# The last attention block of a four-layer kernel: who adds up the exponentials, and in which order TensorE, VectorE and ScalarE finish the block

## The chip, the cores and the metric

One Trainium2 chip, one core of it. The metric is the device time of one launch in microseconds (us); lower is better. The engines are TensorE (PE, its weight loads PEld), VectorE (DVE), ScalarE (ACT), GpSimd (POOL) and SyncE (SP, here the issuer of most transfers).

## The reference, cut to what matters

Four layers with residuals run over x of shape (1, 2048, 128), all in float32:

```python
x = x + L0_attn(layernorm(x))   # 8 heads; softmax over 2048 keys; this layer ends where the change is
x = x + L0_ffn(layernorm(x))    # gate from the MEAN over all 2048 rows of the normalised x, top 2 of 8 experts
x = x + L1_attn(layernorm(x))   # anchors: softmax over 64 anchors, 16 heads
x = x + L1_ffn(layernorm(x))    # top 2 of 8 experts per row
```

Of the first layer:

```python
scores = einsum('bhsd,bhtd->bhst', q, k) * scale
attn = softmax(scores, axis=-1)           # exp(score - row max) / sum over the 2048 keys
o = einsum('bhst,bhtd->bhsd', attn, v_c)
return o.reshape(b, s, H * DK) @ W_O + b_O
```

and of the second, `pooled = x.mean(axis=1); gate = softmax(pooled @ gate_w.T); top_k(gate, 2)`. Nothing of the second layer's experts can be chosen before all 2048 rows are normalised.

## The kernel before, in words

Every engine has its own instruction stream, written out by hand, and streams meet only at semaphores. The first layer is cut into 32 blocks (`NBLK = 32`): 8 heads (outer) by 4 groups of 512 query rows (inner). Block n, head n // 4, does the following, in 8 slots of two key tiles each:

- `scores(n, t)`: one TensorE matmul gives the scores of 128 keys (tile t of 16) by 512 queries; `exponential(n, t)` on ScalarE writes `prob[:, tile, :]`, a ring of 16 tiles, so one whole block fits.
- `weighted` / `weigh(n, tiles)`: `val` times `prob`, 32 output columns per matmul, so four tiles are worked by four matmuls side by side, into bank U. When all 16 are in, `sums(n)` on ScalarE copies the bank to `u_sb[n % 4]`, and `output(n)` on TensorE multiplies by the folded projection into a bank.
- The softmax denominators: for blocks up to 30, GpSimd, VectorE and adding DMAs reduce the 16 `prob` tiles to a `part` buffer, and `totals(n)` sums over partitions with matmuls against `ones_v`; `sums_out(n)` copies to `den_sb`, a small DMA turns it to `den`. For the last block (31), `last_totals(g)`, g = 0 to 3, does the whole sum on TensorE: four groups of four 512-wide matmuls directly over `prob`, accumulated in bank 6. `sums_out(31)` copies the bank to `den_sb`, and `last_denominators()` turns it with four matmuls.
- `denominators(n)` and `accumulate(n)` on VectorE: reciprocal, then X = out * rden + X in four instructions.

The ends of blocks 28 to 31 are each the last word on one quarter (batch b = 0 to 3, 512 rows) of X, so the second layer's normalisation `ln0` starts there, batch by batch: `ln0_stats(b)` (VectorE, 8 instructions), `ln0_pool(b)` (GpSimd: variance plus epsilon, power), `ln0_norm(b)` (VectorE, 4 instructions, writes `hn`), `ln0_pe(b)` (TensorE, 4 transposes), `ln0_act(b)` (ScalarE copies to `hT` and accumulates the row sums `hsum[:, b]`). The mean over all rows is the sum of two parts. For batches 0 to 2, VectorE adds the three columns of `hsum`; that instruction waits for `ln0_act(2)` and stands in front of `ln0_norm(3)` on VectorE. For batch 3, TensorE sums `hn` against `ones_v` directly ("the pooled matmuls", line 1816 of the profile), behind a `spin`, that is, a number of matmuls whose result nobody reads. Then VectorE adds the parts, TensorE forms the gate's logits, VectorE takes the top two, and the experts' weights are picked.

TensorE's order in block 31 before the change: scores 12 and 13; `weighted(31, 0)` (tiles 0 to 7); `last_totals(0)`, `last_totals(1)`; scores 14 and 15; `output(30)`; `last_totals(2)`; `ln0_pe(1)`; `weigh` tiles 8 to 11; `last_totals(3)`; `weigh` tiles 12 to 15; `last_denominators`; `output(31)`; small transposes of the anchors, the gate and `up0`; `ln0_pe(2)`; the eight transposes of `w_out` (line 1781); `anchor_weights(0)` and `(1)` (line 1790); `spin(8)`; the pooled matmuls.

Lines of the profile used below: 1540 scores, 658 exponentials, 1584 `weigh`, 1604 `totals`, 1615 `last_totals`, 1624 `last_denominators`, 1568 `output`, 367 `ln0_pe`, 373 `ln0_act`, 361 `ln0_norm`, 328 and 335 `ln0_stats`, 341 and 343 `ln0_pool`, 1127 `late_sums` (the two wide additions of block 30 on VectorE), 1159 `accumulate`, 1249 the addition of `hsum`, 641 `sums_out(31)`, 721 `anchors_hi`, 1474 `spin`. A float32 matmul appears as two records, so four matmuls of a group are eight.

Of the kernel before, what the change touches and what calls it, by code (L numbers as in the profile page):

```python
# [5 lines left out]
ALU = mybir.AluOpType  # L6
# [12 lines left out]
def build_kernel(nc, d, out):  # L19

    S, D = d["L0_attn_h_t"].shape[1:]
    NT = S // P
    NB = S // BLK
    C = d["L0_attn_W_DQ"].shape[1]
# [8 lines left out]
    with ctx:  # L33
# [6 lines left out]
        ps = ctx.enter_context(nc.psum_tensor("ps", [P, 8, BLK], F32))  # L40
# [359 lines left out]
        u_sb = [sums_sb[:, 0], sums_sb[:, 1]] + [w_oT[:, :, :].rearrange("p h d -> p (h d)")[:, x * BLK:(x + 1) * BLK] for x in range(2)]  # L400
        part = [part_sb[:, 0], part_sb[:, 1]] + [t.rearrange("p (x h) d -> p x (h d)", x=NG) for t in (w_v[:, :, :], hn[:, :, :])]
        with nc.sbuf_tensor("pT", [P, HP, S], F32) as pT:
            pass
# [49 lines left out]
        with nc.Block() as block:  # L453
# [105 lines left out]
            def _(act):  # L559
# [125 lines left out]
                for n in range(NBLK):  # L685
                    for t in range(NT):
# [16 lines left out]
                        if n == NBLK - 1 and t == 10:  # L703
                            ln0_act(act, 0, 3)
                ln0_act(act, 1, 4)
                sums_out(NBLK - 1)
                sums(NBLK - 1)

# [7 lines left out]
                act.copy(up_x[:, :, :], ps[:, 7, :].rearrange("p (j n) -> p j n", j=E // 2)).then_inc(s_upx, 1)  # L716
                ln0_act(act, 2, 3)

# [18 lines left out]
                anchors_hi(0)  # L737
                anchors_hi(1)
                act.wait_ge(s_gv, 2)
                act.activation(g8[:, EXPD, :], g8[:, TOP, :], ACT.Exp, bias=g1[:, 0:1], accum_out=g1[:, 1:2]).then_inc(s_ge, 1)  # L740
# [318 lines left out]
            def _(dve):  # L1059
# [59 lines left out]
                def late_sums(n, j):  # L1119
# [7 lines left out]
                    dve.tensor_tensor(part[n % 4], part[n % 4], prob[:, at:at + NG, :], ALU.add).then_inc(s_pair, 1)  # L1127

                def key_biases(m, bank):
                    heads = slice(4 * m, 4 * (m + 1))  # L1130
                    dve.wait_ge(s_kb_ps, m + 1)
                    dve.tensor_scalar(kcol[:, heads], ps[:, bank, KB_AT + 4 * m:KB_AT + 4 * (m + 1)], unit[:, E_SH:E_SH + 1], None,
                                      ALU.add).then_inc(s_kb, 1)
                    dve.wait_ge(s_kb, 2 * m + 1)
                    dve.tensor_scalar(kcol_m[:, heads], kcol[:, heads], unit[:, M_KEY:M_KEY + 1], None, ALU.mult).then_inc(s_kb, 1)
# [66 lines left out]
                for n in range(NBLK):  # L1202
                    for slot in range(CPB):
# [27 lines left out]
                        if n == NBLK - 1:  # L1231
                            if slot == 0:
                                ln0_norm(dve, 0)
                            elif slot == 3:
                                denominators(n - 2)
                                accumulate(n - 2)
                                ln0_stats(dve, 1)
                            elif slot == 5:
                                ln0_norm(dve, 1)
                            elif slot == 7:  # L1240
                                denominators(n - 1)
                                accumulate(n - 1)
                                ln0_stats(dve, 2)
                ln0_norm(dve, 2)
                denominators(NBLK - 1)
                accumulate(NBLK - 1)
                ln0_stats(dve, 3)
                dve.wait_ge(ln0["hT"], NB + 3)
                dve.tensor_reduce(hsum[:, NB:NB + 1], hsum[:, 0:NB - 1], AX.X, ALU.add).then_inc(s_pooled, 1)
# [209 lines left out]
            def _(pe):  # L1459
# [148 lines left out]
                def last_totals(g):  # L1608

                    n = NBLK - 1  # L1610
                    if g == 0:
                        bank_read(("sums", n))
                    pe.wait_ge(s_exp, NT * n + NG * (g + 1))
                    for x in range(NG):
                        last = pe.matmul(ps[C * x:C * (x + 1), BANK["sums", n], :], ones_v[:, :], prob[:, (NT * n + NG * g + x) % RING, :],
                                         start=(g == 0), stop=(g == NG - 1))
                    if g == NG - 1:
                        last.then_inc(s_ones, 1)
# [82 lines left out]
                for n in range(NBLK):  # L1701
                    for slot in range(CPB):
# [34 lines left out]
                        if slot == 6 and n == NBLK - 3:  # L1737
                            totals(n - 2)
                        if slot == 6 and n == NBLK - 1:
                            last_totals(0)  # L1740
                            last_totals(1)
                        if slot == 1 and n >= 1:
# [5 lines left out]
                        if n == NBLK - 1:  # L1748
# [6 lines left out]
                            elif slot == 7:  # L1755
                                output(n - 1)
                                last_totals(2)
                                bank_read(("norm", 1))
                                ln0_pe(pe, 1, 4)
                                weigh(n, range(2 * NG, 3 * NG))  # L1760
                last_totals(3)
                weigh(NBLK - 1, range(3 * NG, NT))


# [9 lines left out]
                last.then_inc(s_up_ps, 1)  # L1774
                pe.wait_ge(ln0["hT"], NB + 1)
                ln0_pe(pe, 2, 3)

# [34 lines left out]
                anchor_weights(1)  # L1812
                spin(8, 6)
                pe.wait_ge(ln0["hn"], 2 * NT)
# [296 lines left out]
```

## Time and profile before

| | |
|---|---|
| device time, median of 3 runs | 721.29 us (720.11 to 721.71) |
| device time of the profiled execution | 719.99 us |
| its span (first to last instruction) | 718.3 us |
| TensorE busy | 698.3 us (97% of the span) |
| VectorE / GpSimd / ScalarE busy | 582.4 / 563.6 / 460.3 us |
| granted TensorE clock, mean | 0.999 |
| block 31, scores 0 to start of the pooled matmuls | 453.00 to 480.52 us of the span |

Times inside the kernel are counted from the start of the span. The chain that ended last is TensorE for 71% of the span, GpSimd for 11%, VectorE for 7%. A start time of one instruction of an in-order engine subtracted from the next one's gives what the first costs the stream; the busy time of a row can be longer, since neighbours overlap.

### The profile page before, as it was taken

The numbers are of one execution on the slowest core, as the hardware profiler recorded it, in microseconds if no ns is written. First come the engines' busy times: TensorE is split into PE (matmuls) and PEld (weight loads), VectorE is DVE, ScalarE is ACT, GpSimd is POOL, SyncE is SP. The second block draws the span as 40 slices with busy tenths as digits, with TensorE's granted clock in tenths as the row PEclk, the third lists the DMA queues.
The fourth block names the chain that finished last, engine by engine and source line by source line (L and its number), as shares of the span: only waits on it lengthen the run. The fifth ranks groups of instructions, "written<-read, shape, count | busy, mean of one in ns | idle before, by whom it ended". The sixth has DMA issues, their size and how long they took to land.

```text
span 718.3 us, 12481 instructions
## 1 busy us (share of the span) xinstructions
PE 698.3 (97%) x4280; PEld 470.6 (66%) x4280; DVE 582.4 (81%) x1213; ACT 460.3 (64%) x1069; POOL 563.6 (78%) x466
## 2 busy tenths in 40 slices
PE   8999999999999999999999999999899999999997
PEld 7665556566566566566666656476566599778885
DVE  8878888988988898898889888756978536878885
ACT  4357776776776777767767766655677822465553
POOL 6468999999999999999999997415688761446674
PEclk9999999999999999999999999999999999999999
DMA  6313768778678688687687683040000000032431
GB/s 152 93 38 67 146 126 155 132 137 151 124 148 150 116 154 153 113 156 146 121 153 139 133 155 67 1 121 2 1 2 0 2 1 1 1 89 81 141 104 30
DMA packets 42595, 68.34 MB, mean 95 GB/s; under 512 B 14872, under 2 KB 24105, under 8 KB 38692
## 3 DMA queue, kind: packets, MB, share of 16 engines
q0 software_dynamic: 15680, 52.96, 38.8%
q1 hardware_dynamic: 25572, 14.47, 7.6%
q8 instruction: 34, 0.56, 0.3%
q10 hardware_dynamic: 1280, 0.12, 0.1%
q14 instruction: 29, 0.24, 0.1%
HBM read 13.35 MB, written 1.10 MB: 20 GB/s over the span
## 4 chain that ended last, share of the span: by engine, by line
PE 71%; POOL 11%; issue 7%; DVE 7%; DMA 3%; ACT 2%; POOLq 0%; ACTq 0%; DVEq 0%
PE ps L1540 16%; PE ps L1584 15%; PE ps L1526 15%; POOL hid_lo L1055 5%; PE ps L1953 4%; PE ps L1568 4%; POOL nrm L1035 2%; DVE mx L1109 2%; PE ps L1993 2%; PE ps L1995 2%; PE ps L1994 2%; POOL hid L1035 1%; DMA w_v<-prob 1%; PE ps L1604 1%; PE ps L1513 1%
## 5 line engine op out<-in xcount | busy, mean ns | idle before, releaser
L1109 DVE TENSOR_REDUCE mx<-ps 128x1 f32<-128x512 f32 x492 | 303.1, 682 | 47.9 <-PE ps L1526 47.8
L658 ACT ACTIVATE prob<-ps 128x512 f32<-128x512 f32 x512 | 261.8, 627 | 21.3 <-PE ps L1540 16.2
L1540 PE MATMUL ps<-q_cols,key 128*128 128x512 f32 x512 | 210.3, 414 | 2.3 <-ACT prob L658 1.7
L1526 PE MATMUL ps<-key,q_rows 128*128 128x512 f32 x512 | 202.8, 400 | 0.8 <-DVE key L1095 0.4
L1540 PEld LDWEIGHTS ps<-q_cols,key 128*128 128x128 f32 x512 | 95.4, 187 | 73.9 <-issue 34.1
L1584 PE MATMUL ps<-prob,val 128*32 128x512 f32 x1024 | 123.3, 598 | 0.0
L1526 PEld LDWEIGHTS ps<-key,q_rows 128*128 128x128 f32 x512 | 95.7, 188 | 18.8 <-DVE mx L1103 1.4
L960 POOL TENSOR_TENSOR pair<-prob 128x512 f32<-128x512 f32 x60 | 104.8, 1770 | 4.0 <-ACT prob L658 4.0
L946 POOL TENSOR_TENSOR part<-prob 128x512 f32<-128x512 f32 x64 | 96.5, 1820 | 5.7 <-ACT prob L658 5.6
L1055 POOL TENSOR_TENSOR hid_lo<-hid,hid_hi 128x512 fp32r<-128x512 f32 x44 | 61.6, 1409 | 38.6 <-ACT hid_hi L826 38.6
L1584 PEld LDWEIGHTS ps<-prob,val 128*32 128x32 f32 x1024 | 26.7, 109 | 51.1 <-issue 47.4
L946 POOL TENSOR_TENSOR w_v<-prob 128x512 f32<-128x512 f32 x32 | 48.1, 1808 | 4.4 <-ACT prob L658 4.4
L810 ACT ACTIVATE act_g<-ps 128x512 f32<-128x512 f32 x44 | 26.4, 599 | 32.9 <-PE ps L1995 32.6
L946 POOL TENSOR_TENSOR hn<-prob 128x512 f32<-128x512 f32 x28 | 43.5, 1975 | 2.0 <-ACT prob L658 2.0
L1159 DVE SCALAR_TENSOR_TENSOR X<-ps,rden,X 128x128 f32<-128x128 f32 x128 | 36.0, 344 | 7.4 <-PE ps L1568 4.2
L778 ACT ACTIVATE pT<-ps 128x128 f32<-128x128 f32 x128 | 33.7, 278 | 10.6 <-PE ps L1930 10.6
L967 POOL TENSOR_TENSOR part<-part,pair 128x1024 f32<-128x1024 f32 x16 | 39.1, 2445 | 0.0
L1425 DVE TENSOR_TENSOR prod<-ps,act_g 128x512 f32<-128x512 f32 x44 | 30.1, 685 | 10.8 <-PE ps L1995 8.5
L341 POOL TENSOR_SCALAR vare<-mv 128x4 f32<-128x4 f32 x12 | 4.7, 392 | 41.5 <-DVE mv L335 41.2
L639 ACT COPY den_sb<-ps 128x128 f32<-128x128 f32 x31 | 8.3, 266 | 43.4 <-PE ps L1604 42.6
L1993 PE MATMUL ps<-hT_hi,w_hi 128*128 128x512 f32 x88 | 35.5, 403 | 0.0
L1435 DVE TENSOR_TENSOR hid<-g_all,prod 128x512 f32<-128x512 f32 x26 | 30.6, 1177 | 5.0 <-POOL hid_lo L1055 4.2
(301 smaller groups left out, 1319.4 us busy)
## 6 DMA issues: line engine op xcount, KB each, us to landing
part<-prob POOLq DMA_DIRECT2D x16, 1024.0 KB, 7.1
part<-part POOLq DMA_DIRECT2D x14, 512.0 KB, 8.1
w_v<-prob POOLq DMA_DIRECT2D x7, 1024.0 KB, 7.1
hn<-prob POOLq DMA_DIRECT2D x7, 1024.0 KB, 7.0
part<-part POOLq DMA_DIRECT2D x14, 256.0 KB, 7.4
w_v<-w_v POOLq DMA_DIRECT2D x7, 512.0 KB, 8.0
hn<-hn POOLq DMA_DIRECT2D x7, 512.0 KB, 8.0
g_all<-g_rows SPq DMA_DIRECT2D x9, 256.0 KB, 3.2
```

What stands on the lines that cost most here:

```text
L658: act.activation(prob[:, g % RING, :], ps[:, g % 3, :], ACT.Exp, scale=SCALE).then_inc(s_exp, 1)
L778: act.activation(pT[:, 4 * m + q, u * P:(u + 1) * P], ps[:, 6 + m, q * P:(q + 1) * P], ACT.Copy, accum_out=apart[:, 4 * m + q, u:u + 1]).t ...
L946: pool.tensor_tensor(part[n % 4][:, g, :], tiles(n, 2 * g, 1)[:, 0, :], tiles(n, 2 * g + 1, 1)[:, 0, :], ALU.add).then_inc(s_sum, 1)
L960: pool.tensor_tensor(pair[:, j, :], tiles(n, t, 1)[:, 0, :], tiles(n, t + 1, 1)[:, 0, :], ALU.add).then_inc(s_pair, 1)
L967: pool.tensor_tensor(p, p, pair[:, :, :], ALU.add).then_inc(s_sum, 1)
L1055: pool.tensor_tensor(hid_lo[:, n % 4, :], hid[:, n % 2, :], hid_hi[:, n % 4, :].bitcast(F32), ALU.subtract).then_inc(s_hlo, 1)
L1109: dve.tensor_reduce(mx[:, n % 2, c % TPB, at:at + 1], ps[:, BANK["rows", 2 * lin + j], :], AX.X, ALU.max).then_inc(s_mrd, 1)
L1159: last = dve.scalar_tensor_tensor(out=xt, in0=ps[:, BANK["out", n], i * P:(i + 1) * P], scalar=rden[:, n % 2, i:i + 1], in1=xt, op0=ALU.mu ...
L1526: pe.matmul(ps[:, BANK["rows", 2 * lin + j], :], q_rows[:, k, i * P:(i + 1) * P], key[:, h % KBUF, c0:c0 + BLK], start=True, stop=True).th ...
L1540: pe.matmul(ps[:, g % 3, :], key[:, n // NB % KBUF, t * P:(t + 1) * P], q_cols[:, n % NB, :], start=True, stop=True).then_inc(s_sc, 1)
L1584: last = pe.matmul(ps[C * x:C * (x + 1), U, :], val[:, t, :], prob[:, (NT * n + t) % RING, :], start=(t < NG), stop=(t >= NT - NG))
L1993: pe.matmul(out_ps, w[0], x_hi, start=start, stop=False)
```

## The change

- VectorE adds tiles 0 to 3 and 4 to 7 of block 31 (`last_sums(0)`, behind `ln0_norm(1)`), then tiles 8 to 11 (`last_sums(1)`), into `last_part`, which is `part_sb[:, 1]`. Each is one addition of 128 x 2048.
- TensorE's `last_totals` has two groups instead of four: tiles 12 to 15 from `prob`, then `last_part`. Both stand behind all `weigh` calls of the block.
- `output(30)` moves from in front of the last `ln0_pe(1)` and `weigh` calls to behind them.
- ScalarE copies `sums(31)` before `sums_out(31)`.
- `ln0_norm(2)` on VectorE goes from before `denominators(31)` to behind `ln0_stats(3)`; `ln0_pe(2)` on TensorE and `ln0_act(2)` on ScalarE go behind the anchor weights.
- The spin in front of the pooled matmuls is `spin(4)` instead of `spin(8)`.

```diff
--- before.py
+++ after.py
@@ -399,6 +399,7 @@
 
         u_sb = [sums_sb[:, 0], sums_sb[:, 1]] + [w_oT[:, :, :].rearrange("p h d -> p (h d)")[:, x * BLK:(x + 1) * BLK] for x in range(2)]
         part = [part_sb[:, 0], part_sb[:, 1]] + [t.rearrange("p (x h) d -> p x (h d)", x=NG) for t in (w_v[:, :, :], hn[:, :, :])]
+        last_part = part[(NBLK - 1) % 4 - 2]
         with nc.sbuf_tensor("pT", [P, HP, S], F32) as pT:
             pass
         act_g = sb("act_g", [P, 2, BLK])
@@ -703,8 +704,8 @@
                         if n == NBLK - 1 and t == 10:
                             ln0_act(act, 0, 3)
                 ln0_act(act, 1, 4)
+                sums(NBLK - 1)
                 sums_out(NBLK - 1)
-                sums(NBLK - 1)
 
 
                 act.wait_ge(s_an_ps, 1)
@@ -714,7 +715,6 @@
                 act.activation(gate0T[:, :], ps[:, 0, AT_GATE:AT_GATE + E], ACT.Copy, scale=1.0 / S).then_inc(s_an, 1)
                 act.wait_ge(s_up_ps, 1)
                 act.copy(up_x[:, :, :], ps[:, 7, :].rearrange("p (j n) -> p j n", j=E // 2)).then_inc(s_upx, 1)
-                ln0_act(act, 2, 3)
 
                 def anchors_hi(m):
                     act.wait_ge(s_wa_ps, m + 1)
@@ -736,6 +736,7 @@
                     act.copy(w_oT[:, 4 * m:4 * (m + 1), :], ps[:, 1 + m, :].rearrange("p (h n) -> p h n", h=4)).then_inc(s_wo, 1)
                 anchors_hi(0)
                 anchors_hi(1)
+                ln0_act(act, 2, 3)
                 act.wait_ge(s_gv, 2)
                 act.activation(g8[:, EXPD, :], g8[:, TOP, :], ACT.Exp, bias=g1[:, 0:1], accum_out=g1[:, 1:2]).then_inc(s_ge, 1)
                 act.activation(warm[:, :], ones_row[:, 0:1], ACT.Gelu)
@@ -1125,6 +1126,18 @@
                         dve.wait_ge(s_pair, 2 * n + j)
                     dve.wait_ge(s_exp, NT * n + NG * (3 + j))
                     dve.tensor_tensor(part[n % 4], part[n % 4], prob[:, at:at + NG, :], ALU.add).then_inc(s_pair, 1)
+
+                def last_sums(j):
+
+                    n = NBLK - 1
+                    at = [(NT * n + NG * x) % RING for x in range(3)]
+                    if j == 0:
+                        first = prob[:, at[0]:at[0] + NG, :]
+                    else:
+                        first = last_part
+                        dve.wait_ge(s_pair, 2 * n + 1)
+                    dve.wait_ge(s_exp, NT * n + NG * (2 + j))
+                    dve.tensor_tensor(last_part, first, prob[:, at[j + 1]:at[j + 1] + NG, :], ALU.add).then_inc(s_pair, 1)
 
                 def key_biases(m, bank):
                     heads = slice(4 * m, 4 * (m + 1))
@@ -1237,14 +1250,16 @@
                                 ln0_stats(dve, 1)
                             elif slot == 5:
                                 ln0_norm(dve, 1)
+                                last_sums(0)
                             elif slot == 7:
+                                last_sums(1)
                                 denominators(n - 1)
                                 accumulate(n - 1)
                                 ln0_stats(dve, 2)
-                ln0_norm(dve, 2)
                 denominators(NBLK - 1)
                 accumulate(NBLK - 1)
                 ln0_stats(dve, 3)
+                ln0_norm(dve, 2)
                 dve.wait_ge(ln0["hT"], NB + 3)
                 dve.tensor_reduce(hsum[:, NB:NB + 1], hsum[:, 0:NB - 1], AX.X, ALU.add).then_inc(s_pooled, 1)
                 ln0_norm(dve, 3)
@@ -1610,11 +1625,15 @@
                     n = NBLK - 1
                     if g == 0:
                         bank_read(("sums", n))
-                    pe.wait_ge(s_exp, NT * n + NG * (g + 1))
+                        at = (NT * n + 3 * NG) % RING
+                        tiles = prob[:, at:at + NG, :]
+                    else:
+                        pe.wait_ge(s_pair, 2 * n + 2)
+                        tiles = last_part
                     for x in range(NG):
-                        last = pe.matmul(ps[C * x:C * (x + 1), BANK["sums", n], :], ones_v[:, :], prob[:, (NT * n + NG * g + x) % RING, :],
-                                         start=(g == 0), stop=(g == NG - 1))
-                    if g == NG - 1:
+                        last = pe.matmul(ps[C * x:C * (x + 1), BANK["sums", n], :], ones_v[:, :], tiles[:, x, :],
+                                         start=(g == 0), stop=(g == 1))
+                    if g == 1:
                         last.then_inc(s_ones, 1)
 
                 def last_denominators():
@@ -1736,9 +1755,6 @@
                             totals(n - 3)
                         if slot == 6 and n == NBLK - 3:
                             totals(n - 2)
-                        if slot == 6 and n == NBLK - 1:
-                            last_totals(0)
-                            last_totals(1)
                         if slot == 1 and n >= 1:
                             weighted(n - 1, 1)
                         if slot == 1 and n == NBLK - 3:
@@ -1753,13 +1769,13 @@
                                 bank_read(("norm", 0))
                                 ln0_pe(pe, 0, 3)
                             elif slot == 7:
-                                output(n - 1)
-                                last_totals(2)
+                                weigh(n, range(2 * NG, 3 * NG))
                                 bank_read(("norm", 1))
                                 ln0_pe(pe, 1, 4)
-                                weigh(n, range(2 * NG, 3 * NG))
-                last_totals(3)
                 weigh(NBLK - 1, range(3 * NG, NT))
+                output(NBLK - 2)
+                last_totals(0)
+                last_totals(1)
 
 
                 pe.wait_ge(s_exp, NT * NBLK)
@@ -1772,8 +1788,6 @@
                 for j in range(E // 2):
                     last = pe.transpose(ps[:, 7, j * P:(j + 1) * P], up0[:, 2 * j:2 * (j + 1), :].rearrange("p e c -> p (e c)"), ident[:, :])
                 last.then_inc(s_up_ps, 1)
-                pe.wait_ge(ln0["hT"], NB + 1)
-                ln0_pe(pe, 2, 3)
 
                 for m in range(2):
                     for q in range(4):
@@ -1810,7 +1824,9 @@
                 pe.wait_ge(s_an, 3)
                 anchor_weights(0)
                 anchor_weights(1)
-                spin(8, 6)
+                pe.wait_ge(ln0["hT"], NB + 1)
+                ln0_pe(pe, 2, 3)
+                spin(4, 6)
                 pe.wait_ge(ln0["hn"], 2 * NT)
                 for t in range(NT - TPB, NT):
                     last = pe.matmul(ps[:, 0, AT_POOL:AT_POOL + C], hn[:, t, :], ones_v[:, :], start=(t == NT - TPB), stop=(t == NT - 1))
```

## Rows read from the trace of the kernel before

**Rows 1.** The page: the span.

```profile
span 718.3 us, 12481 instructions
```

**Rows 2.** Chain that ended last, in order of time: start, us, what.

```profile
497.56 0.14 issue
```

**Rows 3.** Timeline, TensorE, 463 to 481: start, us, instructions merged.

```profile
463.42 1.92 PE L1584 MATMUL ps<-prob,val 128*32 128x512 f32 x16
465.16 1.90 PE L1615 MATMUL ps<-prob,ones_v 128*32 128x512 f32 x16
466.99 0.73 PE L1540 MATMUL ps<-q_cols,key 128*128 128x512 f32 x2
467.56 1.05 PE L1568 MATMUL ps<-proj,w_oT 128*128 128x128 f32 x8
468.54 1.06 PE L1615 MATMUL ps<-prob,ones_v 128*32 128x512 f32 x8
469.54 0.65 PE L367 MATMUL ps<-ident,hn 128*128 128x128 f32 x4
470.12 1.06 PE L1584 MATMUL ps<-prob,val 128*32 128x512 f32 x8
471.01 1.04 PE L1615 MATMUL ps<-prob,ones_v 128*32 128x512 f32 x8
471.86 1.04 PE L1584 MATMUL ps<-prob,val 128*32 128x512 f32 x8
472.84 1.04 PE L1624 MATMUL ps<-mean_v,den_sb 128*128 128x1 f32 x8
473.75 1.14 PE L1568 MATMUL ps<-proj,w_oT 128*128 128x128 f32 x8
...
475.64 0.60 PE L367 MATMUL ps<-ident,hn 128*128 128x128 f32 x4
476.08 1.04 PE L1781 MATMUL ps<-ident,w_out 128*128 128x128 f32 x8
476.95 1.95 PE L1790 MATMUL ps<-anchors,emb 128*128 128x128 f32 x16
478.74 1.95 PE L1474 MATMUL ps<-ident 128*128 128x128 f32 x16
480.52 0.98 PE L1816 MATMUL ps<-ones_v,hn 128*128 128x32 f32 x8
```

**Rows 4.** Timeline, VectorE; in brackets idle time before and its releaser.

```profile
453.44 4.58 DVE L1127 TENSOR_TENSOR w_v<-w_v,prob 128x2048 f32<-128x2048 f32 x2
...
464.06 1.12 DVE L361 TENSOR_SCALAR hn<-X,mv,rstd 128x128 f32<-128x128 f32 x4 [1.48 <-POOL rstd L343]
...
474.93 1.13 DVE L1159 SCALAR_TENSOR_TENSOR X<-ps,rden,X 128x128 f32<-128x128 f32 x4 [0.82 <-PE ps L1568]
...
477.16 0.12 DVE L1249 TENSOR_REDUCE hsum<-hsum 128x1 f32<-128x3 f32 x1
...
478.72 1.12 DVE L361 TENSOR_SCALAR hn<-X,mv,rstd 128x128 f32<-128x128 f32 x4 [1.44 <-POOL rstd L343]
```

**Rows 5.** Timeline, ScalarE.

```profile
470.72 0.19 ACT L373 ACTIVATION_READ_ACCUMULATOR hT<-ps 128x1 f32 x1
...
472.11 0.59 ACT L641 COPY den_sb<-ps 128x512 f32<-128x512 f32 x1 [1.20 <-PE ps L1615]
...
478.94 0.59 ACT L721 CAST w_a_hi<-ps 128x512 fp32r<-128x512 f32 x1 [0.31 <-PE ps L1790]
```

**Rows 6.** Instructions of line 341, 445 to 485: ns shortest/median/longest, first and last start.

```profile
L341 POOL TENSOR_SCALAR vare<-mv x4: 229/230/2177, 453.6 to 477.3; 128x4 f32<-128x4 f32 x4
```

**Rows 7.** Timeline, TensorE: the first spin, and a gap at 515.7.

```profile
1.59 6.08 PE L1474 MATMUL ps<-ident 128*128 128x128 f32 x28 [1.59 <-POOL ident L872]
...
517.65 0.66 PE L1930 MATMUL ps<-ident,hid 128*128 128x128 f32 x4 [1.94 <-POOL hid L1035]
```

**Rows 8.** Windows: stretch, then PE, PEld, DVE, ACT, POOL busy, granted clock, DMA.

```profile
515.00:518.00 3.00, 1.06 (x7) 0.59 (x6) 2.93 (x5) 2.49 (x13) 2.93 (x3) 1.00 0.00 0
```

## The prediction

> **What bounds the kernel now.** I read the page first: the span is 718.3 us [rows 1] and TensorE is busy for nearly all of it, so only what TensorE does, or waits for, can count. I then followed the chain that ended last through the stretch of the change. From 453 to 480.5 us it is TensorE with hardly a break; its one crossing to another engine in the part I use is the step from VectorE's `hn` to TensorE's transposes, 0.14 us [rows 2]. The timeline of TensorE gives the cost of each step of block 31 as differences of starts [rows 3]. VectorE's and ScalarE's timelines [rows 4, 5] say what else must be ready. Two things are to be seen. First, `output(31)` starts at 473.75 right behind `last_denominators` at 472.84. Secondly, the pooled matmuls start at 480.52, when `spin(8)` is through, but the last `hn` tile was ready at 478.72 + 1.12 = 479.84 [rows 3, 4]: TensorE's queue, not VectorE, sets that start, with 0.68 to spare on VectorE's side. Everything behind 480.52 keeps its instructions and their order, and everything up to 463.42 does too. So the whole forecast is one question: when do the pooled matmuls start after the change?
>
> **Part 1, TensorE up to output(31).** Start at 463.42. I add the steps in the new order, with durations from [rows 3]. A group of four `weigh` or four `ones` matmuls (8 records) costs 0.87 (1.74 for 16 records, 463.42 to 465.16). If a plain matmul follows, it costs 0.09 to 0.13 more (465.16 to 466.99 is 1.83 for 16; 468.54 to 469.54 is 1.00; 471.86 to 472.84 is 0.98).
>
> - `weigh` tiles 0 to 7: 1.83. Two scores: 0.57 (466.99 to 467.56). `weigh` 8 to 11: 1.00. `ln0_pe(1)`: 0.58. `weigh` 12 to 15: 0.98. `output(30)`: 0.98. First group of totals: 0.87. Second group, to its end: 1.04. Sum 7.85, end at 471.27.
> - Now TensorE must wait for ScalarE, which it did not before. ScalarE started its copy 0.06 behind the end of the last group (471.01 + 1.04 = 472.05, copy at 472.11) and took 0.59 [rows 3, 5]. Then 0.14 back to TensorE. `last_denominators` starts at 471.27 + 0.06 + 0.59 + 0.14 = 472.06, against 472.84.
>
> The two groups taken from TensorE are worth 1.74, but 0.79 of wait on the copy takes the place of work that used to hide it, and one more switch to plain matmuls takes the rest. Net gain 0.78: `output(31)` starts at 472.97. The order of ScalarE's two copies costs nothing: `u_sb` is copied while TensorE does `output(30)` and the totals, and it would delay TensorE only if it ended after 472.8; `weigh` 12 to 15 starts at 467.40 by this count and ends at 468.44, and the copy behind it takes 0.6.
>
> **Part 2, the wide additions.** The same operation stands in block 30: two additions of 128 x 2048 in 4.58 us [rows 4]. They ran beside exponentials and `weigh` as they will here. `ln0_norm(1)` ends at 464.06 + 1.12 = 465.18, so the second addition ends at 469.76. TensorE wants it at 470.23; with 0.14 for the crossing, 0.33 is left. `accumulate(30)` comes behind the additions, at about 470, and needs `output(30)`, which now ends at about 469.4. It and `ln0_stats(2)` take 2.23, as the same pair at 474.93 to 477.16 [rows 4], so VectorE is free at 472.2, before it is wanted for `denominators(31)` at about 473.1. GpSimd's pass over batch 2 then ends before 474. These additions are hidden; without the slack each us of delay would be a us of TensorE.
>
> **Part 3, the third normalisation.** `accumulate(31)` starts 0.78 earlier, at 474.15, `ln0_stats(3)` is issued out by 474.15 + 2.23 = 476.38 [rows 4]. Before, `ln0_norm(3)` then waited only for GpSimd. Now comes a chain:
>
> - `ln0_norm(2)`, 1.12: ends 477.50.
> - TensorE: crossing 0.14 gives 477.64. Is TensorE free? From `output(31)` to the transposes of `w_out` are the 1.89 us of 473.75 to 475.64 (`ln0_pe(2)`'s 0.44 is gone from here), so 474.86; these take 0.87 (476.08 to 476.95), so 475.73; the first anchor weights wait for the copy of `up0` on ScalarE, by my count until 475.79; 1.79 for all anchor weights (476.95 to 478.74) gives 477.58 [rows 3]. Both arrive together. Transposes 477.64 to 478.29.
> - ScalarE: the second `anchors_hi` started 1.99 behind the anchor weights' start (478.94 against 476.95) and took 0.59 [rows 3, 5], so it ends at 475.79 + 1.99 + 0.59 = 478.37. `ln0_act` took 0.72 from the end of the transposes to the end of the accumulator read (469.54 + 0.65 = 470.19 to 470.91) [rows 3, 5]; with the short wait behind `anchors_hi` it ends at 479.05.
> - VectorE: the crossing from ScalarE's accumulator read is in no row by itself. Its bounds are nothing and the 0.14 of [rows 2]; I take 0.04, near the 0.04 to 0.06 of the other crossings into ScalarE here. `hsum`'s addition 0.12, then `ln0_norm(3)` 1.12: ends at 480.33. Crossing 0.14: the pooled matmuls can start at 480.47.
> - TensorE itself: transposes 0.44, then `spin(4)`, half of the 1.78 of `spin(8)` (478.74 to 480.52): free at 477.64 + 0.44 + 0.89 = 478.97. It waits 1.5 us.
>
> So the pooled matmuls start at 480.47 instead of 480.52. **The sum is -0.05 us.** The 0.78 gained at `output(31)`, the 0.44 taken out of TensorE's queue and the 0.89 of shorter spin all lie in front of a chain that starts with `ln0_norm(2)` and is as long as all of them together. `ln0_norm(3)` would be free of it were `hsum`'s addition not in front of it.
>
> The other moves are free: the loads of the last layer's weights, behind the same semaphore as `ln0_stats(3)`, start 0.78 earlier, and the next user is far behind them. Of unknown costs, two more switches of TensorE between kinds of matmul may cost 0 to 0.2 together; the four crossings of part 3 might be 0.1 off each, and the accumulator read may or may not be what `hsum` waits for (0.1 less). The likeliest case's own range is -0.3 to +0.5.
>
> Profiled, the kernel took 719.99 for a span of 718.3; the span becomes 718.25 and that execution 719.94. The median of 3 runs is 1.30 above the profiled execution, and I carry that over: 721.29 - 0.05 = 721.2.
>
> **The clock.** The gap of about 1.5 us in front of the pooled matmuls is new. In the gap of 1.94 us in front of 517.65 [rows 7] the granted clock stayed 1.00 [rows 8], the upper level (2.4 GHz), and the transposes behind it took 0.66, as the 0.65 of 469.54 [rows 3]. The Trainium skill, "TensorE: Matmul & The Clock Gate", section "Why this matters for your kernels", warns that a long idle gap between bursts of matmuls sends the array back to half rate, which speaks against a halved spin; by it TensorE behind 480.5 would start at 1.2 GHz, which is the rival priced below. The rows show a longer gap without it.
>
> **Rivals.**
>
> *Part of the gain arrives (faster).* If `hsum`'s wait does not bind, `ln0_norm(3)` waits for GpSimd only: 478.72 - 0.78 = 477.94, ends 479.06, pooled matmuls at 479.20, -1.32 us: 719.97. The code puts the wait there, so the full amount cannot come; a fraction can, if the crossings are shorter. For: TensorE's own queue is 1.5 us ahead. Cases from -0.3 to -1.3, about 720.7.
>
> *The chain through hT is longer than counted (slower).* TensorE and ScalarE both arrive at `ln0_pe(2)` and `ln0_act(2)` within 0.1 us of being free. If the anchor weights or the copies in front of them slip by 0.3 and each crossing costs 0.14, the pooled matmuls start 0.4 to 1.0 late: about 722.0.
>
> *The additions are late (slower, on the other side).* It decides from 0.33 us on. GpSimd's variance step took 2.18 us beside block 30's additions, against 0.23 otherwise [rows 6]: on a shared path one side can be held for 1.95. If each of the new additions were held so, `last_sums(1)` ends 3.9 late, less 0.33: +3.6, 724.9. Against: GpSimd has nothing to do between 464.0 and 471, and block 30's additions, beside that very step, took their 4.58.
>
> *The clock drops.* The first spin of the program took 6.08/28 = 0.217 us per record, against 1.78/16 = 0.111 in the spin at 478.74 [rows 3, 7]. If the 4 us behind 480.5 ran at that pace: +3.9, 725.2.
>
> **How the numbers follow.** Dead heat (-0.3 to +0.5): 0.60. Part of the gain: 0.20. Longer chain: 0.14. Late additions: 0.03. Clock: 0.02. Something else: 0.01. What a measurement of this kernel can tell from no change is about 0.2%, 1.44 us. Even the full gain of 1.32 stays inside it, and so does the longer chain; but medians of 3 runs scatter (720.11 to 721.71 before), and a real -0.8 can be read as -1.5. From the part-gain case, plus scatter, faster 0.11; from the late additions, the clock, and scatter on the longer chain, slower 0.09; same 0.80. The range of 8 in 10 takes the cases from -1.3 to +1.0 with a little scatter: 719.9 to 722.4.
>
> **What the changed profile would show.** `output(31)` at about 473.0, with TensorE idle 0.8 in front of `last_denominators` waiting for `den_sb`; second addition over by 469.8 and no TensorE wait on it; `ln0_pe(2)` at 477.6 released by VectorE or just behind the anchor weights; `hsum`'s addition at 479.1 released by ScalarE, where before it waited for nothing; the pooled matmuls at 480.4 to 480.6, now released by VectorE's `hn` after an idle gap of TensorE instead of by the spin. The prediction is wrong if the pooled matmuls start before 480.1 or after 481.0, or if the stretch behind them changes its length.

## The result: slower, with the pooled matmuls where they were

| | before | after |
|---|---|---|
| median, 18 runs each | 720.95 us | 726.53 us |
| lowest, highest | 719.39, 722.4 | 721.37, 731.43 |
| ratio | | 1.0068, 95% interval 1.005 to 1.0085 |
| profiled execution: span, mean granted clock | 718.3 us, 0.999 | 724.5 us, 0.988 |

(The ratio on record lies at that of the means, 1.0068; that of the medians is 1.0077.) An execution more than 1.5% above the fastest of its kernel is left out of a ratio as disturbed, which happened once, to the 732.52 us of `g_spin7` below. The change makes the kernel slower by 0.7%. The time is outside the stated range, 719.9 to 722.4. Of the 18 executions of the changed kernel, 4 took 721.4 to 721.9 us at a mean clock of 0.997, one 723.3 at 0.995, and the other 13 took 726.0 to 731.4 at 0.982 to 0.988.

The page of the changed kernel, its first lines and the row of the granted clock by slice (tenths of full speed, 9 for 90% or more, 40 slices):

```profile
span 724.5 us, 12435 instructions
...
PEclk9999999999999999999999999988999999999999
```

TensorE's timeline of the changed kernel, from the first `weigh` of block 31 to the picks, which answers to [rows 3] (1599 is `weigh`, 1555 scores, 1634 `last_totals`, 1643 `last_denominators`, 1583 `output`, 1804 the anchor weights, 1489 `spin`, 1832 the pooled matmuls, 1810 the first values of the third layer):

```profile
463.33 1.92 PE L1599 MATMUL ps<-prob,val 128*32 128x512 f32 x16
465.19 0.73 PE L1555 MATMUL ps<-q_cols,key 128*128 128x512 f32 x2
...
468.43 1.16 PE L1583 MATMUL ps<-proj,w_oT 128*128 128x128 f32 x8
469.52 1.07 PE L1634 MATMUL ps<-prob,ones_v 128*32 128x512 f32 x8
470.40 1.04 PE L1634 MATMUL ps<-part,ones_v 128*32 128x512 f32 x8
472.24 1.02 PE L1643 MATMUL ps<-mean_v,den_sb 128*128 128x1 f32 x8 [0.80 <-ACT den_sb L642]
473.12 1.14 PE L1583 MATMUL ps<-proj,w_oT 128*128 128x128 f32 x8
...
477.81 0.60 PE L367 MATMUL ps<-ident,hn 128*128 128x128 f32 x4
478.24 1.06 PE L1489 MATMUL ps<-ident 128*128 128x128 f32 x8
480.45 1.08 PE L1832 MATMUL ps<-ones_v,hn 128*128 128x32 f32 x8 [1.15 <-DVE hn L361]
...
482.49 1.22 PE L1810 MATMUL ps<-w_oT,emb 64*128 64x128 f32 x4
```

The reader is to see two new idle gaps, 0.80 us in front of `last_denominators` and 1.15 in front of the pooled matmuls, the pooled matmuls at 480.45 against 480.52, and in the last row four records that take 1.22 us. In the kernel before the same four, same shapes, read:

```profile
482.47 0.71 PE L1796 MATMUL ps<-w_oT,emb 64*128 64x128 f32 x4
```

VectorE of the changed kernel, against [rows 4]:

```profile
465.01 2.29 DVE L1140 TENSOR_TENSOR part<-prob 128x2048 f32<-128x2048 f32 x1
467.33 2.29 DVE L1140 TENSOR_TENSOR part<-part,prob 128x2048 f32<-128x2048 f32 x1
...
476.53 1.08 DVE L361 TENSOR_SCALAR hn<-X,mv,rstd 128x128 f32<-128x128 f32 x4
479.21 0.16 DVE L1264 TENSOR_REDUCE hsum<-hsum 128x1 f32<-128x3 f32 x1 [1.60 <-ACT hT L373]
479.29 1.11 DVE L361 TENSOR_SCALAR hn<-X,mv,rstd 128x128 f32<-128x128 f32 x4
```

Now the time, cut into three stretches: from the first `weigh` of block 31, from the pooled matmuls to the first up projection (490.32 before, 496.61 after), and the rest. Windows of the kernel before, then of the changed one (columns: stretch, its length, busy us of PE, PEld, DVE, ACT, POOL with instructions, granted clock, DMA share, GB/s):

```profile
463.40:480.50 17.10, 17.10 (x145) 11.00 (x145) 8.21 (x39) 8.37 (x21) 3.53 (x7) 1.00 0.20 57
480.50:490.30 9.80, 9.55 (x68) 7.00 (x66) 4.11 (x18) 4.40 (x11) 0.00 (x0) 1.00 0.46 125
490.30:718.30 228.00, 216.15 (x1167) 168.87 (x1166) 167.20 (x350) 128.62 (x409) 142.88 (x109) 1.00 0.12 36
```

```profile
463.30:480.50 17.20, 15.25 (x122) 9.47 (x121) 12.61 (x41) 8.40 (x21) 3.53 (x7) 1.00 0.23 70
480.50:496.60 16.10, 15.85 (x66) 11.29 (x66) 4.11 (x18) 4.40 (x11) 0.00 (x0) 0.58 0.24 62
496.60:724.50 227.90, 216.15 (x1167) 168.88 (x1166) 167.23 (x350) 128.44 (x409) 142.79 (x109) 0.99 0.12 36
```

All of the loss is in the middle stretch: the same work, 66 weight loads in both, takes 16.10 us instead of 9.80, at a granted clock of 0.58 on average. The same view cut finer shows the edges:

```profile
482.00:482.50 0.50, 0.50 (x5) 0.33 (x5) 0.42 (x4) 0.12 (x1) 0.00 (x0) 0.97 1.20 291
482.50:483.00 0.50, 0.50 (x3) 0.50 (x3) 0.43 (x3) 0.48 (x3) 0.00 (x0) 0.50 1.20 291
...
495.00:496.00 1.00, 1.00 (x2) 0.00 (x0) 0.10 (x1) 0.00 (x0) 0.00 (x0) 0.50 0.00 0
496.00:497.00 1.00, 1.00 (x6) 0.69 (x6) 0.00 (x0) 0.29 (x2) 0.00 (x0) 0.94 0.00 0
```

From 482.5 to about 496.1 TensorE ran at the lower level (0.50, 1.2 GHz), though it was busy throughout; the fall came 2 us after the gap had ended. Just before it, TensorE had idled for 1.15 us and then, after the pooled matmuls, for 0.25 us in front of the gate's logits, which it did in the kernel before too.

### The profile page after: what moved, and what is told of

Read it like the earlier page. It is cut to its first block, busy times and chain, and to the rows that moved or that the text cites. A ratio compares the mean times of both kernels' runs of the same rounds, so it can differ in the third digit from the quotient of the medians.

```text
span 724.5 us, 12435 instructions
## 1 busy us (share of the span) xinstructions
PE 701.7 (97%) x4256; PEld 471.7 (65%) x4256; DVE 586.9 (81%) x1215; ACT 460.1 (63%) x1069; POOL 563.3 (78%) x466
## 4 chain that ended last, share of the span: by engine, by line
PE 72%; POOL 10%; issue 7%; DVE 5%; DMA 3%; ACT 2%; POOLq 0%; ACTq 0%; DVEq 0%
PE ps L1555 17%; PE ps L1599 15%; PE ps L1541 15%; POOL hid_lo L1056 5%; PE ps L1969 4%; PE ps L1583 4%; POOL nrm L1036 2%; PE ps L2009 2%; PE ps L2011 2%; PE ps L2010 2%; DVE mx L1110 1%; POOL hid L1036 1%; DMA w_v<-prob 1%; PE ps L1619 1%; PE ps L1528 1%
```

## The experiments

Theory 1: the new idle gaps of TensorE lower the clock, the one in front of the pooled matmuls above all. Rivals: the new order of the totals, with its wait for `den_sb`, lowers it whatever stands in front of the pooled matmuls; or the gap alone, in the old order, does nothing. Each kernel was timed beside the kernel before on the same chip. "From weigh" is the time from the first `weigh` of block 31 to the pooled matmuls in the profiled execution: it shows what the schedule alone does. "Fall" is the time that the clock stayed at 0.50 behind the pooled matmuls in the profiled execution, worked out from windows of it.

The last two columns count executions by their mean granted clock. The 13 profiles say what that mean stands for: the four with a mean of 0.998 or more show no fall up to 714 us, close to the end of the span, and the nine with 0.997 or less each show one (3.4 us of it: 0.996 or 0.997; 6.8 us: 0.995; 10 us at the start of the program: 0.992; 13.6 us: 0.988; 20.5 us: 0.984). So "high", 0.998 or more, stands for no fall, and "low", 0.989 or less, for a long one or several. Of the 104 executions of the kernel before that ran beside these kernels, 64 were high and none was low; their lowest was 0.991.

| kernel | gaps, us | from weigh, us | fall, us | ratio, 95% interval | high | low |
|---|---|---|---|---|---|---|
| before | none | 17.10 | none | 1 | 64 of 104 | 0 of 104 |
| the change | 0.80 + 1.15 | 17.12 | 13.6 | 1.0068 (1.005 to 1.0085) | 0 of 18 | 13 of 18 |
| a_spin10 | 0.80 | 17.14 | none | 1.0006 (0.9991 to 1.0022) | 5 of 12 | 0 of 12 |
| g_spin7 | 0.80 + 0.48 | 17.12 | 3.4 | 1.0022 (1.000 to 1.0044) | 3 of 12 | 1 of 12 |
| h_spin0 | 0.80 + 2.04 | 17.12 | 20.5 | 1.0081 (1.0051 to 1.0112) | 0 of 6 | 4 of 6 |
| b_spin0 | 0.98 | 16.47 | 3.4 | 1.0036 (1.0016 to 1.0055) | 0 of 12 | 3 of 12 |
| c_sums_only | 0.80 | 16.56 | none | 1.0012 (0.999 to 1.0034) | 5 of 12 | 0 of 12 |
| d_norm_only | 1.15 | 17.67 | 6.8 | 1.0058 (1.0036 to 1.0079) | 0 of 12 | 4 of 12 |
| k_den_spin | 1.15 | 17.05 | none | 1.0042 (1.0023 to 1.0061) | 1 of 12 | 1 of 12 |
| e_hsum_last | 0.80 | 15.93 | none | 0.999 (0.9971 to 1.0009) | 6 of 12 | 0 of 12 |
| f_hsum_spin6 | 0.80 | 16.26 | none | 0.9998 (0.9974 to 1.0022) | 3 of 12 | 0 of 12 |
| i_fill | 0.17 | 16.17 | none | 0.9983 (0.997 to 0.9997) | 9 of 12 | 0 of 12 |
| i_fill_again | 0.17 | 16.16 | none | 0.9985 (0.9968 to 1.0001) | 6 of 12 | 0 of 12 |

**The size of the gap, with the changed order kept.** Three kernels differ from the change in one number (g_spin7 has `spin(7, 6)`, h_spin0 no spin):

```diff
-                spin(4, 6)
+                spin(10, 6)
```

> The changed kernel with ten spin matmuls in place of four in front of the pooled matmuls, nothing else. Theory 1 (the idle gap of 1.15 us that TensorE has there, after the 0.80 us wait for den_sb, makes the clock fall to half about 2 us later): the gap closes, the pooled matmuls start at 480.4 to 480.5 as before, the granted clock stays 1.00 from 482 to 496 and the mean is 0.999; time 720.9, that is 0.2 us around the kernel before. Rival (the clock falls because of the thinner TensorE work of the new order, the 0.80 us wait for den_sb above all, not because of the gap ahead of the pooled matmuls): the clock still falls, time 724 to 727.

> The changed kernel with a spin of seven instead of four: the gap ahead of the pooled matmuls is 0.5 us instead of 1.15, the pooled matmuls start at 480.45 as before. If the share of executions with a fallen clock grows with the gap: between the ten-matmul version (ratio 1.0006) and the change (1.0068), about 1.002 to 1.004. If there is an edge, one of the two.

> The changed kernel without any spin: the gap ahead of the pooled matmuls is 2.0 us, the pooled matmuls start at 480.45. Theory 1: the clock falls at least as often and as early as in the change, ratio 1.007 to 1.010, no execution with a mean clock of 0.999 or more. Rival (the gap is not the cause, what the four spin matmuls do is nothing): as the change, 1.0068.

The pooled matmuls start equally late in all four, 17.12 to 17.14 us after the first `weigh`. Only the gap differs, and the ratio follows it: 1.0006, 1.0022, 1.0068, 1.0081 for no gap there, 0.48, 1.15 and 2.04. The two smallest overlap in their intervals and so do the two largest; the jump between 0.48 and 1.15 us is clear. Theory 1 holds, and the rival falls: a_spin10 has the totals and the wait for `den_sb` exactly as the change, and no low execution. g_spin7 has one low execution, but its profiled one, with a mean of 0.997, shows that the small gap does something too:

```profile
481.41 1.08 PE L1832 MATMUL ps<-ones_v,hn 128*128 128x32 f32 x8 [0.48 <-DVE hn L361]
```

```profile
484.00:486.00 2.00, 2.00 (x13) 1.67 (x12) 1.42 (x6) 1.80 (x4) 0.00 (x0) 0.61 0.34 82
```

h_spin0 is not clearly worse than the change by ratio, but all six of its executions had a mean clock of 0.992 or less (of the change 13 of 18), and in its profile the fall came earlier:

```profile
480.00:482.00 2.00, 1.35 (x8) 1.27 (x8) 0.59 (x3) 0.00 (x0) 0.00 (x0) 0.81 1.14 349
482.00:484.00 2.00, 1.75 (x9) 1.32 (x9) 1.01 (x7) 1.07 (x3) 0.00 (x0) 0.50 1.08 261
```

The profiled execution of a_spin10 happened to be its slowest (725.77 us). Windows of it show where, in the first 20 us of the program, and not in this stretch:

```profile
8.00:20.00 12.00, 11.13 (x42) 7.23 (x43) 7.49 (x32) 5.49 (x13) 5.11 (x16) 0.57 0.54 132
...
482.00:500.00 18.00, 17.11 (x125) 13.66 (x124) 8.58 (x42) 8.25 (x20) 4.22 (x7) 1.00 0.43 122
```

So there is a second place at which the clock can fall, at the start, where all these kernels have the same instructions. It may also explain part of the scatter of the kernel before (up to 726 us, mean clock down to 0.991), though no profile of the kernel before shows it. A third place comes with `i_fill` below.

**The gap alone, in the old order.**

```diff
                 anchor_weights(1)
-                spin(8, 6)
```

> The kernel before without its spin of eight matmuls, nothing else. The pooled matmuls are then released by VectorE's hn at 479.84 and start at 479.98, 0.54 us earlier, behind an idle gap of TensorE of about 1.1 us. Theory 1 (a gap of about 1 us here is enough): the granted clock falls to 0.50 for 10 to 13 us in most executions, time 724 to 727. Rival (the gap alone is not enough, the rest of the new order is needed too): clock stays 0.999, time 720.4.

The schedule gained 0.63 us (16.47 against 17.10), and the time got 0.36% worse. Its profiled execution is one of the mild ones (mean clock 0.997) and shows a short fall:

```profile
479.38 1.08 PE L1815 MATMUL ps<-ones_v,hn 128*128 128x32 f32 x8 [0.98 <-DVE hn L361]
```

```profile
482.00:484.00 2.00, 2.00 (x13) 1.69 (x12) 1.42 (x6) 1.78 (x4) 0.00 (x0) 0.62 1.05 254
484.00:486.00 2.00, 2.00 (x13) 2.00 (x11) 0.15 (x1) 0.00 (x0) 0.00 (x0) 0.53 0.00 0
486.00:488.00 2.00, 2.00 (x13) 1.12 (x12) 0.76 (x2) 0.75 (x2) 0.00 (x0) 1.00 0.04 8
```

So a gap of 1 us in front of the pooled matmuls is enough by itself. My expectation of a fall of 10 to 13 us in most executions was too much: 3 of 12 were low. But all 12 had a mean clock of 0.997 or less, where 64 of 104 of the kernel before had more, so a shorter fall, as in this profile (3.4 us), is likely in most.

**The change in halves.** c_sums_only keeps the additions, the totals and the order of TensorE and takes back the moves of batch 2 and the spin:

```diff
 # VectorE, from the change
+                ln0_norm(dve, 2)
                 denominators(NBLK - 1)
                 accumulate(NBLK - 1)
                 ln0_stats(dve, 3)
-                ln0_norm(dve, 2)
 # TensorE
                 last.then_inc(s_up_ps, 1)
+                pe.wait_ge(ln0["hT"], NB + 1)
+                ln0_pe(pe, 2, 3)
...
                 anchor_weights(1)
-                pe.wait_ge(ln0["hT"], NB + 1)
-                ln0_pe(pe, 2, 3)
-                spin(4, 6)
+                spin(8, 6)
```

(`ln0_act(2)` goes back likewise.) d_norm_only is the other half, the same lines in the other direction, made in the kernel before.

> The changed kernel with the moves of the third normalisation and the shorter spin undone: the wide additions, the two groups of totals, output(30) behind the last weights and the order of the two copies stay; norm, transposes and copy of batch 2 stand where they stood, and the spin has eight matmuls. The wait for den_sb of 0.80 us stays, the gap ahead of the pooled matmuls is gone. Norm of batch 2 on VectorE now waits for GpSimd until about 473.6 and holds accumulate(31) to about 474.8, so little is gained: the pooled matmuls start at about 480.0. Theory 1: granted clock 0.999, time 720.2 to 720.9. Rival (the new order of totals and its wait on den_sb lower the clock): clock falls to 0.50 behind 482, time 724 to 727.

> The kernel before with only the moves of the third normalisation and the spin of four: norm of batch 2 behind the last statistics, its transposes and its copy behind the anchor weights. The chain through hsum then starts 0.78 us later than in the changed kernel: hsum's addition at about 480.0, pooled matmuls at about 481.2, 0.7 us later than before, behind a gap of about 1.2 us. Theory 1: the clock falls as in the changed kernel, time 725 to 728. Rival (the totals and the den_sb wait are needed): clock 0.999, time 721.6.

The first half gains 0.54 us of schedule, as expected, and has no low execution. Its median, 721.37, is no better than that of the kernel before, 721.15: a gain of 0.54 us is below what 12 executions can tell, and it is above the 720.2 to 720.9 that I had expected. The second half costs 0.57 us of schedule by itself (0.7 expected) and brings the gap of 1.15; 4 of 12 executions were low and none was high. The slowdown belongs to the second half.

**Does the wait for den_sb count too?** k_den_spin puts three spin matmuls into it and leaves the later gap:

```diff
+                spin(3, 1)
                 last_denominators()
```

> The changed kernel with three spin matmuls in the 0.80 us wait for den_sb ahead of last_denominators; the gap of 1.15 us ahead of the pooled matmuls stays. If only the later gap counts: ratio as in the change, 1.006 to 1.008. If the two gaps add up: about that of the kernel before without its spin (one gap of 1 us), 1.0036.

1.0042, with 1 low execution of 12 against 13 of 18, and the schedule as before. That points to the two gaps adding up, as does d_norm_only (1.15 alone, 4 of 12); the intervals of the ratios overlap, so it is likely, not shown. With 1 high execution of 12 the clock fell somewhere in nearly every one; what seems rarer with the earlier gap filled is a long fall. Its profiled execution has the gap of 1.15 us and no fall behind it (its 0.996 comes from a later place, see `i_fill`):

```profile
481.11 1.08 PE L1833 MATMUL ps<-ones_v,hn 128*128 128x32 f32 x8 [1.15 <-DVE hn L361]
```

```profile
484.00:486.00 2.00, 2.00 (x20) 1.88 (x17) 1.58 (x7) 1.50 (x4) 0.00 (x0) 1.00 0.19 45
486.00:490.00 4.00, 4.00 (x28) 2.71 (x27) 1.08 (x4) 1.72 (x5) 0.00 (x0) 1.00 0.03 6
```

So a gap of 1.15 us does not lower the clock in every execution.

**Taking hsum out of the chain.** The prediction had named `hsum`'s addition, in front of `ln0_norm(3)`, as what eats the gain. e_hsum_last swaps the two:

```diff
                 ln0_norm(dve, 2)
+                ln0_norm(dve, 3)
                 dve.wait_ge(ln0["hT"], NB + 3)
                 dve.tensor_reduce(hsum[:, NB:NB + 1], hsum[:, 0:NB - 1], AX.X, ALU.add).then_inc(s_pooled, 1)
-                ln0_norm(dve, 3)
```

> The changed kernel with the addition of hsum behind ln0_norm(3) on VectorE instead of in front of it; spin of four. ln0_norm(3) then waits only for GpSimd (478.05) and ends at 479.2, the pooled matmuls start at 479.3 to 479.4, 1.1 us earlier than in the kernel before, and TensorE's gap ahead of them is 0.2 us instead of 1.15. Theory 1 (the gap lowers the clock): clock as in the kernel before, time about 719.9 where no clock falls, ratio 0.997 to 0.999. Rival (four spin matmuls and the new order are too thin whatever the gap): clock still falls, 724 or more.

f_hsum_spin6 is the same with `spin(6, 6)`:

> As e_hsum_last with a spin of six: TensorE is busy until 479.57, so no gap ahead of the pooled matmuls, which start at 479.6, 0.9 us earlier than in the kernel before. Theory 1: clock as in the kernel before, ratio 0.998 to 0.999. Rival (thin order): clock falls.

The schedule is 1.17 and 0.84 us shorter than before, as expected, with no gap in front of the pooled matmuls in either and no low execution. e_hsum_last keeps the four spin matmuls of the change, so it was the gap that lowered the clock and not the small number of them. The ratios, 0.999 and 0.9998, cannot be told from 1.

**Both gaps filled.** i_fill has the swap of e_hsum_last and real work in the wait for `den_sb`:

```diff
+                pe.wait_ge(s_usb, NBLK)
+                pe.transpose(ps[0:A, 0, 0:A], anchor[:, :], ident[0:A, 0:A])
+                pe.transpose(ps[:, 0, AT_GATE:AT_GATE + E], gate0[:, :], ident[0:E, 0:E]).then_inc(s_an_ps, 1)
+                for j in range(E // 2):
+                    last = pe.transpose(ps[:, 7, j * P:(j + 1) * P], up0[:, 2 * j:2 * (j + 1), :].rearrange("p e c -> p (e c)"), ident[:, :])
+                last.then_inc(s_up_ps, 1)
                 last_denominators()
                 output(NBLK - 1)
-                pe.transpose(ps[0:A, 0, 0:A], anchor[:, :], ident[0:A, 0:A])
...
                 anchor_weights(1)
+                spin(3, 6)
                 pe.wait_ge(ln0["hT"], NB + 1)
                 ln0_pe(pe, 2, 3)
-                spin(4, 6)
+                spin(6, 6)
```

> hsum's addition last as in e_hsum_last, and both gaps of TensorE filled: the transposes of the anchors, the gate and up0 go in front of last_denominators, into the 0.80 us wait for den_sb (behind a wait for u_sb), three spin matmuls stand in front of ln0_pe(2), six behind it. TensorE is then busy without a gap from 463 to the pooled matmuls at 479.5, 0.9 to 1.0 us earlier than in the kernel before. Theory 1: clock as in the kernel before, ratio 0.998 to 0.999, and not better than e_hsum_last if a gap of 0.8 and one of 0.2 do nothing; better by up to 0.001 if they matter.

> A repeat of i_fill, whose interval (0.997 to 0.9997) came close to 1. If the gain is real: ratio 0.9975 to 0.9995 again, from 0.9 us less up to the pooled matmuls and fewer executions with a lowered clock. If it was chance: about 1.000.

TensorE's timeline of i_fill, where the 0.80 us wait is gone and one gap of 0.17 is left:

```profile
471.00 1.04 PE L1634 MATMUL ps<-part,ones_v 128*32 128x512 f32 x8
471.98 0.24 PE L1785 MATMUL ps<-ident,anchor 64*64 64x64 f32 x1
...
472.80 1.01 PE L1643 MATMUL ps<-mean_v,den_sb 128*128 128x1 f32 x8
...
478.30 0.63 PE L367 MATMUL ps<-ident,hn 128*128 128x128 f32 x4 [0.17 <-DVE hn L361]
478.77 1.50 PE L1489 MATMUL ps<-ident 128*128 128x128 f32 x12
480.11 0.98 PE L1834 MATMUL ps<-ones_v,hn 128*128 128x32 f32 x8
```

0.9983 and, repeated, 0.9985: medians 719.70 and 720.01 against 720.74 and 720.56. The first interval excludes 1 and the second just reaches it. This version is 0.15% faster than the kernel before and 0.8% faster than the change; the first is within the 0.2% that I had called no change, and is as large as the 0.93 us of its schedule (16.17 against 17.10).

The repeat shows one thing more. The prediction had taken the gap of 1.94 us in front of 517.65 as proof that such a gap is harmless. The two runs are the same program, and their profiled executions differ right there. TensorE's rows and a window, first of i_fill, then of i_fill_again:

```profile
517.22 0.66 PE L1948 MATMUL ps<-ident,hid 128*128 128x128 f32 x4 [1.94 <-POOL hid L1036]
521.26 0.60 PE L1948 MATMUL ps<-ident,nrm 128*128 128x128 f32 x4
518.00:521.00 3.00, 3.00 (x13) 1.90 (x12) 2.10 (x4) 2.84 (x17) 2.37 (x2) 1.00 0.00 0
```

```profile
516.63 0.66 PE L1948 MATMUL ps<-ident,hid 128*128 128x128 f32 x4 [1.94 <-POOL hid L1036]
522.33 0.60 PE L1948 MATMUL ps<-ident,nrm 128*128 128x128 f32 x4
518.00:521.00 3.00, 3.00 (x9) 1.86 (x8) 1.54 (x3) 2.40 (x13) 1.78 (x1) 0.50 0.00 0
```

In the second the clock fell for 3.4 us, and the way to the next transposes took 5.70 us instead of 4.04: a short fall costs 1.7 us. The same gap is followed by the same fall in the profiles of f_hsum_spin6 and k_den_spin (1.95 us, 5.71 and 5.69), three of 13 in all.

## Why the prediction was wrong

Its own question, when the pooled matmuls start, was answered rightly, step by step; times below in us, predicted and measured, the measured ones being 0.09 earlier from the start (463.33 against 463.42).

| step | predicted | measured |
|---|---|---|
| second addition ends | 469.76 | 467.33 + 2.29 = 469.62 |
| wait for `den_sb` in front of `last_denominators` | 0.79 | 0.80 |
| `output(31)` starts | 472.97 | 473.12 |
| `ln0_norm(2)` ends | 477.50 | 476.53 + 1.08 = 477.61 |
| `ln0_pe(2)` starts | 477.64 | 477.81 |
| `hsum`'s addition starts | 479.09 | 479.21 |
| `ln0_norm(3)` ends | 480.33 | 480.40 |
| pooled matmuls start | 480.47 | 480.45 |
| TensorE idle in front of them | 1.5 | 1.15 |

- **Part 1.** The gain at `output(31)` was 0.78 predicted; from the first `weigh` it is 10.33 before (473.75 - 463.42) and 9.79 after, 0.54. `output(30)` behind the last weights took 1.09 instead of 0.98, and the two scores 0.66 (465.19 to 465.85) instead of 0.57; the wait for `den_sb` was right. The size is a bit off, the mechanism right.
- **Part 2.** Right. The additions took 2.29 each, and TensorE did not wait for them. The rival of late additions did not occur.
- **Part 3.** Right. The chain through `hsum` gave back what had been gained, and e_hsum_last showed the other side of it: with the swap the pooled matmuls come 1.17 us earlier, as the rival "part of the gain arrives" had worked out in full (1.32).
- **"Everything behind 480.52 keeps its instructions and their order."** True, but I took from it that the stretch keeps its length. It took 6.30 us more.
- **"The clock."** This is the step that failed. I had seen the new gap and taken one gap of 1.94 us at 517.65, with no fall behind it [rows 7, 8], for proof that 1.5 us is harmless, and gave the rival a chance of 0.02. That one execution proves nothing even for its own place: behind the same gap the clock fell in 3 of the 13 profiles, and in one of two executions of the same program (i_fill and i_fill_again). In place of "harmless" the runs showed: with a gap of about 1 us the clock falls in most executions (59 of 60 with a gap of 0.98 us or more had a mean clock of 0.997 or less, against 40 of 104 of the kernel before), and it stays down for 3.4 to 13.6 us, 20.5 behind the gap of 2.04. Why it is short in one execution and long in another stays open.
- **The price of that rival** was +3.9 us, on a guess that the low clock lasts for 4 us. It lasted 13.6 us (482.5 to 496.1), and work that took 9.80 us took 16.10: +6.3 in the profiled execution, +5.6 in the median. The rival's 725.2 is near the measured 726.53, but with a length that was a guess.
- **"spin(4), half of spin(8)".** I booked the eight spin matmuls of before as a wait in TensorE's queue, 0.68 us too long. They also kept TensorE busy up to the release of the pooled matmuls. Taking out four (0.89), with all that stands in front of them 0.54 earlier and the release where it was, is what opened the gap. (It is 1.15 and not the predicted 1.5 because `ln0_pe(2)` started 0.17 late and the last spin matmul ends 0.17 behind the half of `spin(8)` that I had counted.)

The Trainium skill, "TensorE: Matmul & The Clock Gate", section "Why this matters for your kernels", warns of idle gaps between bursts of matmuls; the prediction cited it and set it aside. The gaps that it warns of are longer than any here, so by its words the 1.15 us gap was no danger either; the measurement decides. The runs agree with its direction: the clock went to the lower of its two levels (1.2 GHz) after gaps of 0.48 to 2.04 us, and in the profile of a_spin10, with the gap closed, it stayed at 1.00.

## What to carry to other kernels

Matmuls that nobody reads, just ahead of a wait, may be there for the clock: before they are shortened or anything is moved away from their side, work out the idle time that is left, and price it at the lower clock over the dense stretch behind it (here 1.7 us for a short fall, 6.3 for that of the change). When a chain on another engine gets longer under TensorE, give TensorE as much filler as the chain needs (here ten matmuls instead of four: 1.0068 became 1.0006), or better, take the link out of the chain (`hsum` behind the last normalisation) and put real work in the remaining wait (0.9983). And a question of clock is settled over many executions, with each one's mean granted clock, never by one profile.

## What the runs showed of the hardware that was not expected

- The clock fell 2.0 us after the gap had ended (480.45 to 482.5), in the midst of work, and stayed at 0.50 for 13.6 us with TensorE busy throughout. In the other profiles it fell 0.6 us (h_spin0) to 3.1 us (b_spin0) after the end of the gap in front of the pooled matmuls and stayed down for 3.4 us (b_spin0, g_spin7), 6.8 (d_norm_only) or 20.5 (h_spin0).
- The same program with the same gap of 1.94 us had a fall behind it in one execution (i_fill_again) and none in another (i_fill).
- Without a gap in front of the pooled matmuls about half of the executions had a mean clock of 0.998 or more (64 of 104 of the kernel before, 5 of 12 of a_spin10); with a gap of 0.98 us or more 1 of 60 had (the change, h_spin0, b_spin0, d_norm_only, k_den_spin). How many falls were long followed the size up to 1.15 us: 0 of 12, 1 of 12 at 0.48 us, 13 of 18 at 1.15, 4 of 6 at 2.04, all with the 0.80 us gap some 8 us before.
- The clock can also be low in the first 20 us of the program (0.57 from 8 to 20 us in the profile of a_spin10), for some 5.8 us of the time: block 31's first `weigh` stood at 469.10 there and at 463.33 in the changed kernel.
